# Zero fills behind each expert's last row: sixteen in one place, or four in each of four places

## What is computed

```
gate_logits = x @ gate_w + gate_b
topk_vals, topk_idx = jax.lax.top_k(gate_logits, K)          # K = 2 of 16 experts
topk_w = jax.nn.softmax(topk_vals, axis=-1)
h = jax.nn.relu(jnp.einsum('bsh,ehf->bsef', x, w1) + b1)
expert_out = jnp.einsum('bsef,efh->bseh', h, w2) + b2
sel = jnp.take_along_axis(expert_out, topk_idx[:, :, :, None], axis=2)
moe = jnp.sum(topk_w[..., None] * sel, axis=2)
y = x + moe                                                   # then a layer norm over the row
```

## Time and profile before

| | us |
|---|---|
| median of 3 runs | 1520.53 |
| lowest and highest of them | 1517.84 and 1522.57 |
| the profiled execution, in all | 1516.08 |
| its span, from the first to the last instruction | 1514.2 |
| around the span | 1.9 |
| TensorE busy in the span | 1137.3 (75%) |
| VectorE busy | 1030.5 (68%) |
| POOL busy | 1040.8 (69%) |

### The profile page before, as it was taken

One profiled execution on the slowest core, in us unless ns is written; L12 is line 12 of the kernel. 1 busy time (PEld: TensorE's weight loads), 2 busy tenths in 40 slices (PEclk: granted clock), 3 DMA queues, 4 the chain that ended last, 5 costly groups with the idle time before them and its releaser, 6 DMA issues. The chain is left out here.

```text
span 1514.2 us, 34216 instructions
## 1 busy us (share of the span) xinstructions
PE 1137.3 (75%) x10594; PEld 986.1 (65%) x10594; DVE 1030.5 (68%) x3731; ACT 452.7 (30%) x1286; POOL 1040.8 (69%) x1068
## 2 busy tenths in 40 slices
PE   2338999667768988888888987887978878596930
PEld 2327788556557877777777876776867767575820
DVE  7863666577787767676675767665666566694767
ACT  3763455222222322222222222232222223221310
POOL 3657777767757777777777777777777776442535
PEclk9999999887778999999998999999989899798975
DMA  8238777544456666556555555566555555587965
GB/s 258 75 101 268 243 252 251 183 129 141 155 156 162 162 160 160 160 149 167 159 155 157 154 161 158 148 170 164 147 154 155 149 151 151 145 207 189 251 182 168
DMA packets 214482, 257.79 MB, mean 170 GB/s; under 512 B 92690, under 2 KB 177382, under 8 KB 213994
## 3 DMA queue, kind: packets, MB, share of 16 engines
q0 software_dynamic: 47328, 128.21, 31.0%
q1 hardware_dynamic: 149978, 111.76, 25.6%
q10 hardware_dynamic: 16992, 15.47, 3.3%
HBM read 179.45 MB, written 64.86 MB: 161 GB/s over the span
## 5 line engine op out<-in xcount | busy, mean ns | idle before, releaser
L1108 POOL DMA_INDIRECT ring<-ytab,src x782 | 778.1, 995 | 259.3 <-issue 234.1
L2069 PE MATMUL agg<-ring,oh 128*128 128x256 f16 x2346 | 313.5, 287 | 104.4 <-DMA ring<-ytab,src 104.4
L2069 PEld LDWEIGHTS agg<-ring,oh 128*128 128x128 f16 x2346 | 260.5, 117 | 137.1 <-issue 117.8
L2171 PE MATMUL H<-misc,big 128*128 128x128 f16 x2448 | 203.6, 229 | 0.3
L2171 PEld LDWEIGHTS H<-misc,big 128*128 (+1 forms) x2448 | 172.1, 102 | 15.9 <-issue 2.0
L2187 PE MATMUL OB<-big,misc 128*128 (+1 forms) x1224 | 156.2, 279 | 0.0
L814 POOL DMA_INDIRECT ring<-ytok,slot x74 | 73.3, 991 | 92.5 <-DMA out<-ring 50.6
L1116 POOL DMA_INDIRECT disp<-misc,slot x98 | 103.8, 1059 | 47.6 <-issue 45.4
L2187 PEld LDWEIGHTS OB<-big,misc 128*128 128x128 f16 x1224 | 119.5, 100 | 16.9 <-issue 0.2
L1590 DVE TENSOR_TENSOR oh<-eq,whl 128x1024 f16<-128x1024 f16 x196 | 127.1, 690 | 3.4
L1814 DVE SCALAR_TENSOR_TENSOR misc<-H,misc 128x512 f16<-128x512 f32 x102 | 70.3, 689 | 59.3 <-ACT misc L1312 57.8
(11 more groups left out here) (282 smaller groups left out, 2365.9 us busy)
## 6 DMA issues: line engine op xcount, KB each, us to landing
ytok<-misc ACTq DMA_DIRECT2D x118, 128.0 KB
ring<-ytab,src POOLq DMA_INDIRECT x782
big<-in_w1p SPq DMA_DIRECT2D x15, 512.0 KB, 4.2
big<-in_w2p SPq DMA_DIRECT2D x15, 512.0 KB, 6.3
big<-in_x_pt SPq DMA_DIRECT2D x7, 896.0 KB, 12.1
ytab<-big SPq DMA_DIRECT2D x7, 896.0 KB, 4.1
selfr<-ytab SPq DMA_DIRECT2D x49, 128.0 KB
xtd<-misc SPq DMA_DIRECT2D x49, 128.0 KB, 6.0
```

Source lines behind the costliest of these rows:

```text
L1108: e.indirect_dma_start(ring[:, (c % R) * 512:(c % R) * 512 + 512], None, ytab[0:NP, :], bass.IndirectOffsetOnAxis(ap=src[:, c:c + 1], axis ...
L2069: m_ = e.matmul(o_, oh[:, g % 2, wp, (c % 8) // 4, :, c % 4], ring[:, a_ + 256 * yp:a_ + 256 * yp + 256], start=False, stop=True, skip_gro ...
L2171: m_ = e.matmul(o_, ws(h * 1024 + wp * 512 + f * 128, 128), zp[:, h * 128:h * 128 + 128], start=False, stop=(h == 1 and q == 2))
```

## The change

`fill_ends` takes a number q and issues only four of the fills, with one register load that fills four registers. It is called in the slots 1, 3, 5 and 7 of the drain, behind the flips of the slot and ahead of its stores. The copy of `tailt` to `endoff` leaves `ends()` and stands ahead of the drain's first slot. It has an increment of `left` of its own, so that `left` counts to 4: `endoff` is 2, `tailoff` 3, `flag` 4. Nothing else in the computation differs.

```diff
@@ settled
-        e.wait_ge(S["left"], 3)
+        e.wait_ge(S["left"], 4)
@@ SP
-            freg = e.alloc_register(name="fill")
-
-            def fill_ends():
+            fregs = [e.alloc_register(name=f"fill{i}") for i in range(4)]
+
+            def fill_ends(q):
                 on.wait_ge("left", 2)
-                for x in range(EXP):
-                    e.reg_load([freg], endoff[0:1, x:x + 1])
-                    e.dma_start(disp[bass.ds(e.snap(freg, min_val=0, max_val=EXP * CAP - P), P), :],
+                e.reg_load(fregs, endoff[0:1, 4 * q:4 * q + 4])
+                for r in fregs:
+                    e.dma_start(disp[bass.ds(e.snap(r, min_val=0, max_val=EXP * CAP - P), P), :],
                                 A["zrows"][0:P, :]).then_inc(S["fill"], 16)
@@ SP, the drain
-                if k == ND - 5:
-                    fill_ends()
+                if j % 2 and j // 2 < 4:
+                    fill_ends(j // 2)
                 final_stores(j - 1)
@@ VectorE, ends()
-                then(e.tensor_copy(endoff[:, :], tailt[0:1, :]))
@@ VectorE, ahead of the drain
             on.wait_ge("seen", NT)
+            own.wait_ge(hold["tail"])
+            e.tensor_copy(endoff[:, :], tailt[0:1, :]).then_inc(S["left"], 1)
             for j, k in enumerate(TAILK):
```

## The result

| | before | changed |
|---|---|---|
| median of the runs, us | 1520.62 (4 runs) | 1507.42 (4 runs) |
| lowest and highest | 1517.84 and 1522.57 | 1506.32 and 1508.27 |
| profiled execution, us | 1516.08 | 1506.32 |
| its span | 1514.2 | 1504.5 |

The ratio of the times is 0.9914, with a 95% interval from 0.9897 to 0.9931: 13.2 us faster by the medians. The forecast was 1505.4, within 1499 to 1513.

A forecast was written before the change was run, and what follows sets the result against it. SP's sixteen fills held back the flip that TensorE needed in the drain, whose end sets the kernel's end. 10.9 + 4.8 - 0.6 = 15.1 us saved from the median of 1520.5 gave 1505.4 us, range 1499 to 1513.

The forecast's parts named there:

- Term 1: Item 101 to 102: the flip of item 102 no longer waits behind the fills; 10.9 us saved, bounds 10 and 11.
- Term 2: Items 102 to 117: 3.35 us per item instead of 3.67; 4.8 us saved, bounds 2.6 and 10.1.
- Term 3: Slots 1, 3, 5, 7: SP's four added groups of fills might stall TensorE once; -0.6 us, bounds 0 and -5.7.
- the chance of one in ten: Early drain: chance of one TensorE stall, if SP's backlog and a flip's landing are both at their worst; -0.6 us.
- the room behind the groups: Early drain: SP has 1.5 us of room per two slots, paying the groups' backlog back by about slot 16.
- who waits: Behind the groups: the flips of items 95 to 98, and the stores with their loads; flips 8.4 and 9.3 us ahead.
- Rival 1: Whole drain: the DMA engines set the pace instead; 10.0 us saved, 1510.5 us; chance 0.20.
- Rival 2: Whole drain: TensorE alone sets the pace; 21.0 us saved, 1499.5 us; chance 0.12.
- Rival 3: Slots 2 to 8: late flips stall TensorE; 7.1 us slower, 1527.6; chance 0.05 slower, 0.05 for stalls that eat the gain.
- Rival 4: Item 102: another condition of its flip is as late, so nothing is gained; 1520.5 us; chance 0.03.
- The rule on the order within a ring: SP's queue: descriptors go in ring order, so flips behind a group land later, moving the groups' cost towards -5.7 us.
- price of 5.7 us for one stall: TensorE in the drain: one stall costs 2.83 us idle plus 2.85 us at the slow clock.

The follow-up runs named there:

- Burst12: The changed kernel with its four groups of fills called together in slot 12, behind the flip of item 101; ratio 0.9980 to the kernel before.
- the repeat: The changed kernel run again, nothing altered; drain 124.9 us, ratio 0.9918 to the kernel before.
- burst1: The changed kernel with all four groups of fills in slot 1; ratio 0.9941 to the kernel before.
- wide: The changed kernel with fills of 256 rows instead of 128, the same number of instructions; ratio 0.9916 to the kernel before.
- two8: The changed kernel with two fills in each of the slots 0 to 7 instead of four in each second slot; ratio 0.9919 to the kernel before.

## Why the prediction was right, point by point

**What bounds the kernel before.** Right. The drain's end sets the kernel's end, and behind it the length stayed (57.5 to 58.9 us in all 14 profiles). The three waits for flips before the change come to 16.3 us, not 13.9 in two: the earlier trace rows shows one line of two. Burst12 shows that what held item 102 was the burst's length on SP: a burst 4.2 us shorter made B 3.6 us shorter.

**Term 1, 10.9 us.** Right, 11.3 measured (14.9 to 3.6), in every kernel with early fills. But not for the reason of comfort that I gave. I had the flip of item 102 going out at 1369.2 and SP with 4.8 us in hand. It went out as the second of the pair at 1375.35, at 1377.08, 5 us later than that after the later start of this drain is taken off. With a slow landing it would just have been late at the place that I had in mind. What saved it is that item 102 itself came later, by what A lost.

**Term 2, 4.8 us, bounds 2.6 and 10.1.** The size was within its bounds: 6.5 in one execution, 3.2 in the next (C = 48.6 and 51.9), 3.24 and 3.46 us per item for the 3.35 that I took. The limit was the right one: SP's flips from items 101 and 102 to 116 and 117 took 1425.73 - 1375.35 = 50.4 us for 15 items, 3.36 each, and TensorE went at 3.0 on its lead until item 110, whose flip came 1.7 us late. The lower bound of 3.00 was reached only without the loads of the finals.
But the gain did not come where I saw it. 4.0 us of it are item 102 to 103, the burst's after-effect, which I had spread over 15 items. From item 103 on the pace was 3.44 us before and 3.26 and 3.50 in the two executions after: no gain is shown there. That the term came out near its size is in part luck.

**Term 3, -0.6 us, bounds 0 and -5.7.** This is the term that was mis-sized: A lost 3.1 and 3.4 us. Three steps of it failed.
The first is the chance of one in ten. I had SP at most 6.3 us late, and the flip of item 97 with a lead of 9.3 us, 3.3 to spare with a slow landing. These figures together already say that it comes 3 us late, or just in time with a landing of 3 us. I called that both at their worst, and it was the regular case. The flip went out at 1360.47 instead of 1351.19, 6.7 us late after the later start is taken off, was 5.3 us under way, and TensorE waited 1.41 us for it, 1.9 in the repeat. The chain that ended last has it:

```profile
1360.47 5.26 DMA misc<-disp
```

The second is the room behind the groups. SP had 10.2 us of waits for other engines in A before, 1.0 after: the room was there, and the groups used it up. Then I held SP's fastest pair of slots, 6.40 us, against TensorE's 7.93, and had the backlog paid back by slot 16. SP's pairs behind the last group took 1367.53 - 1360.47 = 7.1 and 1375.35 - 1367.53 = 7.8 us, without a wait for another engine. There was next to no room, so SP stayed late until the static items.
The third is who waits. I named the loads behind the groups and priced only the flips. The first stall, 1.24 us ahead of item 94's second layer, came by way of VectorE: its sum had waited 1.36 us for a load, and `hidden_lo` stood behind it. The 2.85 us wait at 1364.8 is the same kind; it fell into TensorE's wait for the flip of item 97 and cost nothing more.
The group itself was over-priced: 0.31 + 2.8 = 3.1 us instead of 3.6.

**The sum.** 11.3 + 6.5 - 3.1 is 14.7, against 15.1 forecast. Stretch D, which I had left out, took 1.5 us of it, 0.7 in the repeat: the last hidden values and the last write to `ytok` came a little later in a busier drain. The drain gained 13.2 us, 10.3 in the repeat; the medians moved by 13.2 and, in the repeat's runs, by 12.7. That the sum came so close is luck in part: term 3 was too small by 2.5 us and D was left out, and term 2 in this one execution was larger by 1.7.

**The rivals.** Rival 1, the DMA engines' bytes, is out as it was put: 2.1 MB more and 2.75 MB less left the drain at 123.8 and 123.5. That its 121.5 us were nearly met by the changed kernel's 122.0 is a coincidence. Rival 2, TensorE alone, needs the loads away. Rival 3, stalls behind the groups, happened on a small scale, two short waits in A, three in the repeat, and not three of 5.7 us; burst1 is its stronger form and still 0.6% faster than before. Rival 4 is out with B = 3.6.
The rule on the order within a ring that I held against the change is neither borne out nor contradicted: fills landed in 3.1 us at the median, 2.8 before, and wide, with twice the bytes in front of the flips, cost 0.6 to 0.9 us in A. What a flip loses by standing behind fills is below that, and no run takes it apart.

## What to carry to other kernels

An engine that only issues DMAs is a resource like any other: add up its instructions per step, at their usual and not their fastest time, and hold them against the step of the engine that it feeds. A block of independent DMAs belongs where a lead of several items still stands between it and the next consumer, spread so that each piece is shorter than that lead (that the spreading itself paid is likely here and not shown), and everything that stands behind it in the queue has to be priced, the loads as well as the flips. How late the queue will be and how long a transfer is under way have to be added up and held against the lead: both at once is the regular case. When one wait of 11 us is removed, look at once for what has run without slack beside it: here 7 us of the drain are held by loads for which VectorE had waited only 3.4 us before.

## What the runs showed of the hardware that I had not expected

The length of a wait of TensorE alone does not tell what its clock does after it. In the kernel before, 2.83 us idle ahead of item 110 were followed by 5.9 us at a clock of 0.50, half of 2.4 GHz. In the repeat of the changed kernel the engine waited 3.03 us at the same item, and the clock stayed at 1.00. In both the clock had been 1.00 for nearly 10 us ahead of the wait, with the engine busy. TensorE's row of the repeat and the windows behind the waits, first of the kernel before:

```profile
1422.30:1428.20 5.90, 5.84 (x42) 5.04 (x43) 5.09 (x16) 0.60 (x1) 3.30 (x4) 0.50 1.13 308
```

```profile
1411.69 0.23 PE L2169 MATMUL agg<-sel,bank 80*128 80x128 bf16 x1 [3.03 <-DMA misc<-disp]
```

```profile
1411.60:1414.60 3.00, 2.91 (x41) 2.77 (x42) 2.90 (x11) 0.60 (x1) 0.46 (x1) 1.00 0.95 314
```

Nor does a longer wait fare worse in the other kernels: after 2.47 us at item 110 (burst1) the clock stayed at 1.00, after 2.34 us at item 114 (two8) it was 0.63 on average for the next 4.6 us. What decides it these runs don't show. My price of 5.7 us for one stall, half of it slow clock, was therefore too high for most of them.

Also not expected: one register load that fills four registers takes SP 0.31 us, hardly more than the 0.27 us of a load of one.
